# Two graph attention layers: layer 0's context as three fp32r products of split parts, and a new order of the mixed phase

## The chip, the cores and the metric

The kernel runs on one core of a Trainium2 chip. The metric is the device time of one launch, in microseconds. The core has five engines with an instruction list each: TensorE (PE, matrix products; its weight loads are shown as PEld), VectorE (DVE), ScalarE (ACT), GpSimd (POOL) and SyncE (SP, which here issues all DMAs). Every engine follows its own list strictly in order and waits on semaphores; while one instruction waits, all that stand behind it on that engine wait as well.

## The reference, cut to what matters

There are 16 graphs of N = 512 nodes with D = 256 channels. `x` is (16, 512, 256), `adj` is (16, 512, 512) with entries 0 and 1. Two layers follow each other.

Layer 0 has one head of width 256:

```
q = x @ Wq + bq;  k = x @ Wk + bk
scores = q k^T / 16, -1e18 where adj == 0
attn = softmax(scores), 0 where adj == 0
ctx = (attn @ x) @ Wc
x = layer_norm(x + ctx) * gamma + beta
```

Layer 1 has 8 heads of width 32, and the logarithm of the clipped adjacency is added to its scores (the kernel multiplies the exponentials by the clipped adjacency instead, which is the same):

```
logits = q k^T / sqrt(32) + log(clip(adj, 1e-8))
out = softmax(logits) @ v, heads joined, @ Wo^T + bo
x = layer_norm(x + out) * gamma + beta
```

All is in float32. The kernel keeps that accuracy in two ways: with matrix products of type fp32, or by splitting each operand into a high part (fp32r, a rounded form) and a low part (the rest), and adding up the three products high by high, high by low and low by high in fp32r.

## The kernel before, in words

**Tiles.** A graph has T = 4 row tiles of 128 nodes and C = 2 halves of the channels. Layer 1's eight heads form GROUPS = 2 groups of four; its 32 score tiles of 128x512 are handled as 8 quads (quad = 4*group + row tile) of two pairs of heads each.

**Phases.** The work is a software pipeline over the graphs. One pass of the loop, a "mixed phase", does three things at once: the front of graph j (layer 0, and layer 1's projections and row maxima), the back of graph i = j-1 (layer 1's attention), and the tail of graph t = i-1 (output projection, second norm, store). `run` (L424) issues a first phase (front only), one phase without a tail, 14 full phases as a loop over i from 1 to 14, then a last phase (no front) and an end (tail only).

**Order.** Inside a phase the order is written out by hand as a list of stages: FIRST, SCHEDULE (the mixed phases) and LAST, L61 to L115. Each engine walks the same list (`follow`) and does its own part of each stage that it knows, so the list fixes the order on all engines. A stage in the list such as ("scores1", 2, 1) makes TensorE compute two score tiles, ScalarE take their exponentials, and GpSimd multiply the pair by the clipped adjacency (L1146), unless ("mask", 2, 1) is in the list: then VectorE does this multiplication (L991) where "mask" stands.

**Banks.** Four PSUM banks ("misc") serve the stages in MISC_DRAIN in turn. The stage that fills a bank waits until the stage four uses earlier has been drained, by ScalarE or by VectorE as the table says. Two further banks hold layer 1's scores, one its summed values (PV), one its denominators (DEN); the last two also hold the output projection. Layer 1's weights have three SBUF buffers `PR`, so quad n's exponentials wait until quad n-3 has been summed.

**The stages that matter here**, with the lines of the profile:
- split: ScalarE casts the transposed x to its high part XTH (L806), VectorE subtracts (XTL, L954).
- q0: six matmuls (L600), ScalarE writes Q0H (L811), VectorE Q0L (L970). q1 and k1 likewise, for layer 1.
- u: rows of x @ Wc, six fp32r matmuls of 258 columns (L610); ScalarE copies them to U (L822).
- bias: VectorE makes the 0/1 array ABSENT from the adjacency (L983). max0: a row bound of layer 0's scores, matmuls L652 and L654, VectorE reduces (L995). floor, shift0: ScalarE and VectorE turn this into the shift NM0 (L827, L1001, L834).
- scores0: eight matmuls of 512 columns (L665, L669, L670), then ScalarE's exponential into P0 (L838).
- context0: per tile four fp32 matmuls of P0 by U, 257 columns (L678); VectorE divides by the sum in column 0, adds x and takes statistics (L1022 to L1030). stats0: GpSimd computes 1/std (L1135, L1137). norm0: VectorE writes xn (L1045). transpose: L687, parts XNH (ScalarE, L873) and XNL (VectorE, L964). v: L622, copied by ScalarE (L816). residual: two GpSimd operations (L1129, L1131).
- max1 (g, n): one 32-row matmul (L700) and one VectorE reduction of 128x512 (L1006), 16 for each group. mrow1 (g): TensorE turns the 16 columns of maxima (L705), VectorE copies (L1012), and a DMA puts them into the stacks QS. clip: L979.
- scores1 (L721), values1 and denominators1 (L744), sums_v, sums_w (ScalarE, L857, L863), reciprocal (L1053), normalise (L1059), high_output (ScalarE, L868), low_output (L1063), and project (24 matmuls, L766; VectorE adds the residual, L1072). The projection's first tile has its four products with the high part first and waits for low_output of group 1 only before its sixth matmul. stats1, norm1, output: VectorE L1078 to L1088, GpSimd L1135, L1137, L1160, L1162.

SP copies the parts of q1 and k1 into the stacks, 24 DMAs for each group, and issues the loads for the next graph between them; it is a queue in order as well.

## Time and profile before

| | |
|---|---|
| time, median of 3 runs | 1230.44 us (1230.1 to 1231.08) |
| time of the profiled execution | 1230.28 us |
| its span, first to last instruction | 1228.5 us |
| its mean granted TensorE clock | 0.974 |
| busy share TensorE, VectorE, GpSimd, ScalarE | 93%, 76%, 60%, 43% |

The span is what the profile's views divide up; the time has 1.8 us around it. Times in the rows are microseconds from the start of the span unless marked ns. In the order-of-time views, matmuls in a row are merged: "x8" is eight records, and the length given is that of the merged row. Ends of matmuls are modelled and overlap what follows, so a stage's cost is read from its start to the start of the next stage. A matmul of type fp32 leaves two records. An entry in brackets is the idle time of the engine ahead of the row and what ended it.

### The profile page before, as it was taken

The page shows a single profiled execution, that of the slowest core. Times are in us where ns is not written, and L with a number is a line of the kernel's source. Part 1 is how long each engine was busy: PE and PEld are TensorE (multiplying, and loading weights), DVE is VectorE, ACT ScalarE, POOL GpSimd, SP SyncE. Part 2 cuts the span into 40 slices and gives each one's busy share as a digit, 9 for nine tenths or more (in the row PEclk, how much of TensorE's full clock was granted, in tenths as well). Part 3 has the DMA queues.
Part 4 walks back from the last instruction along what each step waited for, and adds up shares of the span by engine and source line. Part 5 has one row for each costly group of instructions (what it writes and reads, how often), then busy time and mean ns, then how long its engine had stood idle before and what let it go on. Part 6 is the DMA issues. An engine that isn't in the chain of part 4 may idle for free.

```text
span 1228.5 us, 21300 instructions
## 1 busy us (share of the span) xinstructions
PE 1148.0 (93%) x6474; PEld 686.1 (56%) x6474; DVE 934.6 (76%) x1735; ACT 523.5 (43%) x1020; POOL 734.1 (60%) x352
## 2 busy tenths in 40 slices
PE   6879999999999999999999999999999999999883
PEld 5656465655646565564656556465656646565431
DVE  4465887968778796877879687887968788796874
ACT  1224454444345444434544443444444344444431
POOL 0007568474956847485784748577474857757462
...
GB/s 129 0 115 58 66 107 39 137 32 123 66 85 87 43 140 23 126 62 92 79 45 143 17 128 60 96 80 44 140 17 131 57 100 86 37 137 17 87 34 17
DMA packets 69652, 94.67 MB, mean 77 GB/s; under 512 B 14081, under 2 KB 32769, under 8 KB 69634
## 3 DMA queue, kind: packets, MB, share of 16 engines
...
q14 instruction: 8, 0.07, 0.0%
...
## 4 chain that ended last, share of the span: by engine, by line
PE 40%; DVE 23%; POOL 18%; issue 12%; ACT 5%; DMA 1%; DVEq 0%; POOLq 0%; ACTq 0%; SPq 0%
PE misc L600 11%; DVE mx L1006 8%; POOL PR L1146 8%; PE scores L721 6%; PE misc L622 4%; PE misc L610 3%; POOL z L1160 3%; POOL res L1129 3%; PE misc L652 2%; PE misc L700 2%; DVE PR L991 2%; PE values L744 2%; PE values L766 2%; DVE K1L L970 2%; DVE sums_w L1053 2%
## 5 line engine op out<-in xcount | busy, mean ns | idle before, releaser
L1146 POOL TENSOR_TENSOR PR<-PR,CLIP 128x1024 f32<-128x1024 f32 x217 | 543.0, 2527 | 373.3 <-ACT PR L850 373.3
L1006 DVE TENSOR_REDUCE mx<-misc 128x1 f32<-128x512 f32 x512 | 322.6, 681 | 92.9 <-PE misc L700 92.6
L850 ACT ACTIVATE PR<-scores 128x512 f32<-128x512 f32 x512 | 279.3, 602 | 226.5 <-PE scores L721 217.9
L721 PE MATMUL scores<-QS,KS 97*128 97x512 f32 x512 | 196.4, 461 | 8.9 <-issue 3.5
L744 PE MATMUL values<-PR,V 128*32 128x512 f32 x1024 | 133.2, 604 | 14.5 <-DVE PR L991 14.4
L744 PE MATMUL denominators<-PR,ones 128*32 128x512 f32 x1024 | 133.7, 605 | 0.8 <-DVE z L1072 0.3
L721 PEld LDWEIGHTS scores<-QS,KS 97*128 97x128 f32 x512 | 89.7, 193 | 68.1 <-ACT PR L850 36.1
L700 PE MATMUL misc<-K1H,Q1H 32*128 32x512 f32 x512 | 119.7, 502 | 6.4 <-DVE K1L L970 1.6
L678 PE MATMUL misc<-U,P 128*128 128x257 f32 x512 | 121.8, 386 | 0.0
L1053 DVE RECIPROCAL sums_w<-sums_w 128x128 f32<-128x128 f32 x128 | 114.1, 925 | 6.9 <-ACT sums_w L863 4.0
L700 PEld LDWEIGHTS misc<-K1H,Q1H 32*128 32x128 f32 x512 | 48.4, 184 | 119.1 <-DVE mx L1006 63.7
L678 PEld LDWEIGHTS misc<-U,P 128*128 128x128 f32 x512 | 94.6, 189 | 19.8 <-issue 3.8
L838 ACT ACTIVATE P<-misc 128x512 f32<-128x512 f32 x64 | 38.3, 598 | 96.3 <-PE misc L670 96.3
L744 PEld LDWEIGHTS values<-PR,V 128*32 128x32 f32 x1024 | 25.2, 109 | 68.9 <-issue 44.6
L991 DVE TENSOR_TENSOR PR<-PR,CLIP 128x1024 f32<-128x1024 f32 x39 | 59.8, 1538 | 1.9 <-ACT PR L850 1.8
L665 PE MATMUL misc<-Q0H,XTH 128*128 128x512 f32 x128 | 59.0, 461 | 0.0
L816 ACT COPY V<-misc 128x512 f32<-128x512 f32 x32 | 18.7, 585 | 89.5 <-PE misc L622 89.5
L1135 POOL TENSOR_TENSOR ve<-mv,eps 128x4 f32<-128x4 f32 x32 | 6.4, 202 | 83.0 <-DVE mv L1037 59.3
L1160 POOL TENSOR_TENSOR z<-z,spread 128x1024 f32<-128x1024 f32 x16 | 38.3, 2391 | 28.9 <-DVE z L1088 28.9
L970 DVE SCALAR_TENSOR_TENSOR Q1L<-misc,cols,Q1H 128x512 fp32r<-128x512 f32 x32 | 24.0, 751 | 39.8 <-ACT Q1H L811 39.8
L744 PEld LDWEIGHTS denominators<-PR,ones 128*32 128x32 f32 x1024 | 22.4, 108 | 52.6 <-issue 46.1
L665 PE MATMUL misc<-Q0L,XTH 128*128 128x512 f32 x128 | 51.0, 398 | 0.0
...
## 6 DMA issues: line engine op xcount, KB each, us to landing
...
QS<-Q1H SPq DMA_DIRECT2D x256, 64.0 KB, 2.0
KS<-K1H SPq DMA_DIRECT2D x256, 64.0 KB, 2.0
...
QS<-Q1L SPq DMA_DIRECT2D x128, 64.0 KB, 2.0
KS<-K1L SPq DMA_DIRECT2D x128, 64.0 KB, 2.0
...
```

Source lines behind the costliest of these rows:

```text
L600: mm = pe.matmul(bank[:], w[:, k, P * c:P * (c + 1)], s[:, k, :], start=(n == 0), stop=(n == len(terms) - 1))
L665: pe.matmul(bank[:], kk[:, c, rows_k], qq[:, c, :], start=(n == 0), stop=False)
L678: mm = pe.matmul(bank[:, 0:D + 1], P0[:, k, P * t:P * (t + 1)], U[:, k, 0:D + 1], start=(k == 0), stop=(k == T - 1))
L700: pe.matmul(bank[:], Q1H[part, g, P * t:P * (t + 1)], K1H[part, g, :], start=True, stop=True).then_inc(misc_filled, 1)
L721: pe.matmul(ST[n][:], KS[:, h, P * k:P * (k + 1)], QS[:, h, :], start=True, stop=True).then_inc(scores_filled, 1)
L744: mm = pe.matmul(bank[DK * h:DK * (h + 1), :], w, PR[quad % WEIGHT_BUFFERS][:, h, :], start=(k == 0), stop=(k == T - 1))
L850: act.activation(PR[quad % WEIGHT_BUFFERS][:, h, :], ST[n][:], ACT.Exp, scale=SCALE1).then_inc(exp_done, 1)
L991: dve.tensor_tensor(w, w, clipped, ALU.mult).then_inc(masked_dve, 1)
L1006: dve.tensor_reduce(mx1[:, g, h, t:t + 1], misc_bank(ph, "max1", g, n)[:], AX.X, ALU.max, negate=True).then_inc(misc_drained["dve"], 1)
L1053: dve.reciprocal(sums_w[:, q], sums_w[:, q]).then_inc(back_step, 1)
L1146: pool.tensor_tensor(w, w, clipped, ALU.mult).then_inc(masked_pool, 1)
L1160: pool.tensor_tensor(z[:], z[:], all_rows(S_G1), ALU.mult).then_inc(pool_step1, 1)
```

## The change

Layer 0's context becomes three fp32r products of high and low parts. P0H is the exponential a second time, written as fp32r by ScalarE; its low part is P0 less P0H, computed by GpSimd in a new stage low0 (two operations of 128x1024), and put where XNH and XNL lie, which are free at that time. UH is written by ScalarE in place of U, and UL by VectorE (PSUM less UH), so that the stage u is now drained by VectorE. context0 has 12 matmuls of 258 columns per tile in place of four of 257: four of P0H by UH, four of P0H by UL, four of the low weights by UH, and in the first tile two waits for GpSimd stand before the last group. The list of the mixed phase is reordered throughout; the mask of (3, 0) moves from GpSimd to VectorE. FIRST gains the two low0 stages, LAST is as it was.

```diff
 FIRST = [
...
-    ("scores0", 0), ("scores0", 1), ("prepare", 0), ("scores0", 2), ("scores0", 3), ("prepare", 1),
+    ("scores0", 0), ("scores0", 1), ("low0", 0), ("prepare", 0), ("scores0", 2), ("scores0", 3), ("low0", 1), ("prepare", 1),
...
 SCHEDULE = [
-    ("reciprocal", 1, 0), ("skip_back",), ("split", 0), ("split", 1), ("max1", 1, 0), ("reciprocal", 1, 1),
-    ("max1", 1, 1), ("q0", 0), ("q0", 1), ("scores1", 0, 0), ("bias",), ("u", 0), ("reciprocal", 1, 2),
-    ("scores1", 0, 1), ("u", 1), ("scores1", 1, 0), ("reciprocal", 1, 3), ("u", 2), ("max0", 0),
-    ("normalise", 1), ("scores1", 1, 1), ("max0", 1), ("u", 3), ("high_output", 1), ("max0", 2),
-    ("scores1", 2, 0), ("low_output", 1), ("max0", 3), ("max1", 1, 2), ("max1", 1, 3), ("scores1", 2, 1),
-    ("floor",), ("project",), ("skip_back",), ("max1", 1, 4), ("max1", 1, 5), ("shift0",), ("max1", 1, 6),
-    ("stats1",), ("max1", 1, 7), ("values1", 0), ("values1", 1), ("max1", 1, 8), ("max1", 1, 9),
-    ("denominators1", 0), ("scores0", 0), ("scores0", 1), ("skip_back",), ("output",), ("scores0", 2),
-    ("scores1", 3, 0), ("scores0", 3), ("norm1",), ("max1", 1, 10), ("residual",), ("max1", 1, 11),
-    ("max1", 1, 12), ("denominators1", 1), ("denominators1", 2), ("max1", 1, 13), ("max1", 1, 14),
-    ("max1", 1, 15), ("context0", 0), ("scores1", 3, 1), ("mrow1", 1), ("context0", 1), ("context0", 2),
-    ("scores1", 4, 0), ("values1", 2), ("scores1", 4, 1), ("mask", 4, 0), ("context0", 3),
-    ("scores1", 5, 0), ("denominators1", 3), ("sums_w", 0), ("stats0",), ("norm0",), ("reciprocal", 0, 0),
-    ("values1", 3), ("denominators1", 4), ("reciprocal", 0, 1), ("scores1", 5, 1), ("sums_v", 0),
-    ("transpose", 0), ("mask", 5, 0), ("scores1", 6, 0), ("values1", 4), ("transpose", 1),
-    ("scores1", 6, 1), ("skip_front",), ("values1", 5), ("reciprocal", 0, 2), ("reciprocal", 0, 3),
-    ("q1", 0), ("k1", 0), ("normalise", 0), ("scores1", 7, 0), ("denominators1", 5), ("max1", 0, 0),
-    ("max1", 0, 1), ("max1", 0, 2), ("scores1", 7, 1), ("q1", 1), ("high_output", 0), ("max1", 0, 3),
-    ("max1", 0, 4), ("max1", 0, 5), ("denominators1", 6), ("clip",), ("values1", 6), ("max1", 0, 6),
-    ("max1", 0, 7), ("k1", 1), ("max1", 0, 8), ("denominators1", 7), ("max1", 0, 9), ("max1", 0, 10),
-    ("values1", 7), ("max1", 0, 11), ("max1", 0, 12), ("max1", 0, 13), ("v", 0), ("max1", 0, 14),
-    ("sums_w", 1), ("max1", 0, 15), ("low_output", 0), ("v", 1), ("mrow1", 0), ("sums_v", 1),
+    ("reciprocal", 1, 0), ("split", 0), ("split", 1), ("max1", 1, 0), ("max1", 1, 1), ("max1", 1, 2),
+    ("bias",), ("q0", 0), ("reciprocal", 1, 1), ("scores1", 0, 0), ("reciprocal", 1, 2), ("u", 0),
+    ("scores1", 0, 1), ("q0", 1), ("scores1", 1, 0), ("reciprocal", 1, 3), ("u", 1), ("u", 2),
+    ("scores1", 1, 1), ("max1", 1, 3), ("normalise", 1), ("max0", 0), ("u", 3), ("high_output", 1),
+    ("scores1", 2, 0), ("max0", 1), ("max0", 2), ("low_output", 1), ("max1", 1, 4), ("max1", 1, 5),
+    ("floor",), ("max0", 3), ("project",), ("scores1", 2, 1), ("shift0",), ("skip_back",), ("stats1",),
+    ("max1", 1, 6), ("max1", 1, 7), ("max1", 1, 8), ("denominators1", 0), ("scores0", 0), ("output",),
+    ("scores0", 1), ("scores0", 2), ("denominators1", 1), ("low0", 0), ("skip_back",), ("norm1",),
+    ("values1", 0), ("max1", 1, 9), ("scores0", 3), ("max1", 1, 10), ("max1", 1, 11), ("max1", 1, 12),
+    ("scores1", 3, 0), ("max1", 1, 13), ("low0", 1), ("max1", 1, 14), ("scores1", 3, 1), ("residual",),
+    ("max1", 1, 15), ("context0", 0), ("mrow1", 1), ("context0", 1), ("skip_front",), ("values1", 1),
+    ("context0", 2), ("mask", 3, 0), ("scores1", 4, 0), ("denominators1", 2), ("scores1", 4, 1),
+    ("mask", 4, 0), ("context0", 3), ("denominators1", 3), ("stats0",), ("values1", 2), ("scores1", 5, 0),
+    ("norm0",), ("mask", 5, 0), ("sums_w", 0), ("values1", 3), ("scores1", 5, 1), ("denominators1", 4),
+    ("sums_v", 0), ("transpose", 0), ("values1", 4), ("scores1", 6, 0), ("reciprocal", 0, 0),
+    ("transpose", 1), ("scores1", 6, 1), ("values1", 5), ("reciprocal", 0, 1), ("reciprocal", 0, 2),
+    ("q1", 0), ("reciprocal", 0, 3), ("scores1", 7, 0), ("k1", 0), ("scores1", 7, 1), ("q1", 1),
+    ("denominators1", 5), ("max1", 0, 0), ("max1", 0, 1), ("denominators1", 6), ("normalise", 0),
+    ("high_output", 0), ("max1", 0, 2), ("max1", 0, 3), ("max1", 0, 4), ("max1", 0, 5),
+    ("denominators1", 7), ("max1", 0, 6), ("skip_back",), ("clip",), ("values1", 6), ("max1", 0, 7),
+    ("max1", 0, 8), ("low_output", 0), ("max1", 0, 9), ("k1", 1), ("values1", 7), ("max1", 0, 10),
+    ("sums_w", 1), ("max1", 0, 11), ("v", 0), ("max1", 0, 12), ("max1", 0, 13), ("max1", 0, 14),
+    ("max1", 0, 15), ("v", 1), ("sums_v", 1), ("mrow1", 0),
 ]
...
-    "q0": "dve", "u": "act", "max0": "dve", "scores0": "act",
+    "q0": "dve", "u": "dve", "max0": "dve", "scores0": "act",
...
-                for k in range(T):
-                    mm = pe.matmul(bank[:, 0:D + 1], P0[:, k, P * t:P * (t + 1)], U[:, k, 0:D + 1],
-                                   start=(k == 0), stop=(k == T - 1))
+                terms = [(w, u, k) for w, u in ((P0H, UH), (P0H, UL), (None, UH)) for k in range(T)]
+                for n, (w, u, k) in enumerate(terms):
+                    if t == 0 and w is None and k % 2 == 0:
+                        pe.wait_ge(weights0_low, ph.j * 2 + k // 2 + 1)
+                    q = slice(P * t, P * (t + 1))
+                    mm = pe.matmul(bank[:, 0:D + 2], w[:, k, q] if w is not None else P0L[k][:, q], u[:, k, 0:D + 2],
+                                   start=(n == 0), stop=(n == len(terms) - 1))
...
             def exp0(ph, k):
                 wait_filled(act, ph, "scores0", k)
+                act.activation(P0H[:, k, :], misc_bank(ph, "scores0", k)[:], ACT.Exp, scale=SCALE0)
                 act.activation(P0[:, k, :], misc_bank(ph, "scores0", k)[:], ACT.Exp,
                                scale=SCALE0).then_inc(misc_drained["act"], 1)
...
+            def context_rows_low(ph, t):
+                dve.wait_ge(u_high, ph.j * T + t + 1)
+                dve.tensor_tensor(UL[:, t, 1:1 + D + 2], misc_bank(ph, "u", t)[:, 0:D + 2],
+                                  UH[:, t, 1:1 + D + 2].bitcast(F32), ALU.subtract).then_inc(misc_drained["dve"], 1)
...
+            def weights_low(ph, half):
+                pool.wait_ge(misc_drained["act"], misc.count(ph, "act", "scores0", 2 * half + 1))
+                k = slice(2 * half, 2 * half + 2)
+                pool.tensor_tensor((XNH, XNL)[half][:], P0[:, k, :], P0H[:, k, :].bitcast(F32),
+                                   ALU.subtract).then_inc(weights0_low, 1)
```

## Rows read from the trace of the kernel before

**Rows 1.** The page's first part: busy time of each engine over the span.
```profile
PE 1148.0 (93%) x6474; PEld 686.1 (56%) x6474; DVE 934.6 (76%) x1735; ACT 523.5 (43%) x1020; POOL 734.1 (60%) x352
```

**Rows 2.** Stretches: start:end, length, busy time of each engine, granted clock, DMA.
```profile
604.76:676.10 71.34, 69.43 (x404) 41.46 (x400) 56.87 (x107) 32.29 (x63) 46.89 (x23) 1.00 0.29 81
643.53:655.50 11.97, 11.72 (x76) 6.17 (x68) 11.29 (x18) 3.05 (x6) 1.65 (x1) 1.00 0.68 191
655.50:669.55 14.05, 13.45 (x77) 9.85 (x77) 13.88 (x18) 9.73 (x21) 8.11 (x4) 1.00 0.41 100
```
The engines stand in the order PE, PEld, DVE, ACT, POOL.

**Rows 3.** Order of time of TensorE: start, length, engine, line, operation.
```profile
618.32 3.74 PE L678 MATMUL misc<-U,P 128*128 128x257 f32 x16
...
622.45 1.07 PE L744 MATMUL values<-PR,V 128*32 128x512 f32 x8
623.45 0.73 PE L721 MATMUL scores<-QS,KS 97*128 97x512 f32 x2
624.02 1.90 PE L678 MATMUL misc<-U,P 128*128 128x257 f32 x8
...
634.46 1.07 PE L744 MATMUL values<-PR,V 128*32 128x512 f32 x8 [0.95 <-DVE PR L991]
635.46 0.73 PE L600 MATMUL misc<-XNH,Wq_high 128*128 128x512 f32 x2
...
638.32 0.64 PE L721 MATMUL scores<-QS,KS 97*128 97x512 f32 x2
...
641.24 0.63 PE L600 MATMUL misc<-XNH,Wq_high 128*128 128x512 f32 x2
...
656.33 1.02 PE L600 MATMUL misc<-XTH,A_high 128*128 128x512 f32 x2 [0.51 <-ACT XTH L806]
...
659.51 0.63 PE L721 MATMUL scores<-QS,KS 97*128 97x512 f32 x2
...
661.76 0.41 PE L610 MATMUL misc<-Wc_high,XTH 128*128 128x258 f32 x2
...
662.49 0.68 PE L721 MATMUL scores<-QS,KS 97*128 97x512 f32 x2
...
669.44 0.40 PE L766 MATMUL values<-Wo_high,OTH 128*128 128x256 f32 x2
...
672.38 0.51 PE L700 MATMUL misc<-K1H,Q1H 32*128 32x512 f32 x4
```

**Rows 4.** Order of time of VectorE, the same columns.
```profile
629.12 1.38 DVE L1045 TENSOR_SCALAR xn<-X,mv,rstd 128x256 f32<-128x256 f32 x4 [1.41 <-POOL rstd L1137]
...
643.53 0.75 DVE L970 SCALAR_TENSOR_TENSOR Q1L<-misc,cols,Q1H 128x512 fp32r<-128x512 f32 x1 [1.07 <-ACT Q1H L811]
...
648.98 3.67 DVE L1006 TENSOR_REDUCE mx<-misc 128x1 f32<-128x512 f32 x6
...
665.52 1.22 DVE L1059 TENSOR_TENSOR sums_v<-sums_v,sums_w 128x512 f32<-128x512 f32 x1
...
667.95 1.60 DVE L1063 TENSOR_TENSOR OTL<-sums_v,OTH 128x512 fp32r<-128x512 f32 x1
```

**Rows 5.** Groups by line (busy us, mean ns); then two lines' durations (ns min/median/max).
```profile
L838 ACT ACTIVATE P<-misc 128x512 f32<-128x512 f32 x64 | 38.3, 598 | 96.3 <-PE misc L670 96.3
L964 DVE TENSOR_TENSOR XNL<-misc,XNH 128x512 fp32r<-128x512 f32 x32 | 21.0, 657 | 1.3 <-ACT XNH L873 1.3
L991 DVE TENSOR_TENSOR PR<-PR,CLIP x39: 1161/1226/3155, 124.1 to 1201.0; 128x1024 f32<-128x1024 f32 x39
L1059 DVE TENSOR_TENSOR sums_v<-sums_v,sums_w x32: 676/683/1237, 140.5 to 1208.8; 128x512 f32<-128x512 f32 x32
```

**Rows 6.** Order of time of GpSimd.
```profile
605.51 0.20 POOL L1135 TENSOR_TENSOR ve<-mv,eps 128x4 f32<-128x4 f32 x1 [0.42 <-DVE mv L1083]
...
613.46 2.37 POOL L1146 TENSOR_TENSOR PR<-PR,CLIP 128x1024 f32<-128x1024 f32 x1
...
661.45 12.69 POOL L1146 TENSOR_TENSOR PR<-PR,CLIP 128x1024 f32<-128x1024 f32 x5 [16.27 <-ACT PR L850]
```

22 lines of the change are left out of this document (14 added, 8 removed).

## The prediction

> **What bounds the kernel now.** I read the views in this order. The page's first part says that TensorE is busy for 93% of the span, VectorE for 76%, GpSimd for 60%, ScalarE for 43% [rows 1]. The loop repeats itself, so one mixed phase stands for all: 71.3 us, with TensorE busy 69.4 of them, VectorE 56.9, ScalarE 32.3, GpSimd 46.9, and the granted clock at 1.00 [rows 2]. Read so, TensorE is the bound and two microseconds of idle time are left. But every engine follows its list in order, so an engine with an idle share can still hold the others through a run in which it never rests. I therefore read TensorE and VectorE in order of time [rows 3, 4] and mark four points of a phase:
> - X, the first q1 matmul: 635.46.
> - VectorE starts the second q1 low part: 643.53, or X + 8.1.
> - VectorE ends low_output of group 1 (its last work before the projection): 667.95 + 1.60 = 669.55.
> - P, the first stage behind the projection: 672.38, and one period of 71.34 earlier 601.04. From there to X are 34.4 us.
>
> 8.1 + 26.0 + 2.8 + 34.4 = 71.3, the period. In the 26.0 VectorE is busy for 11.29 + 13.88 = 25.2 [rows 2]. The projection starts on TensorE at 669.44, 0.1 us before low_output ends: there both engines are the bound together.
>
> **What the change removes.** context0 is four fp32 matmuls of 257 columns per tile, each seen as two records. Two tiles and the scores1 behind them take 618.32 to 622.45; less 0.57 for the scores1 (as 623.45 to 624.02) and halved, 1.78 us a tile [rows 3]. The new form is 12 fp32r matmuls of 258 columns. Six of that kind are the stage u, 661.76 to 662.49, so 0.122 us each [rows 3]; twelve make 1.46, and with 0.07 for the change of stage 1.53. The saving is 0.25 us a tile, 1.0 a graph, 16 us over 16 graphs if TensorE alone set the time. The two new waits cost no more than 0.1 us each where the low part is there.
>
> **What it adds.** ScalarE: four more exponentials a graph, into fp32r. No row has one; the f32 one is 0.60, VectorE's 128x512 into fp32r 0.66, both as bounds [rows 5]; I take 0.65. ScalarE has 39 us free in a phase, and a scores0 tile of eight 512-column matmuls takes TensorE 1.9 (q1 0 and k1 0, twelve of them, 635.46 to 638.32), so 1.3 us of exponentials keep up. VectorE: four subtractions a graph of 128x258, PSUM less SBUF. Bounds: 0.34 us (xn, 256 columns, four in 1.38) and 0.66 (128x512 from PSUM into fp32r) [rows 4, 5]; it is half the columns of the second with a fixed part, so nearer the first: 0.37, 1.5 us a graph. One more mask, (3, 0), costs VectorE 1.2 to 1.8 us and frees GpSimd of 2.4 to 2.5 [rows 5, 6]. GpSimd gains two subtractions of 128x1024, which I price as its other operations of that size: 2.37 alone, 2.54 in a row of masks (12.69 for five) [rows 6]; I take 2.38. Sums over a phase: VectorE about 60 us, GpSimd 49, ScalarE 35, all under the period. By shares nothing stands against the saving. The order does.
>
> **The four pieces in the new order.**
> *From X to the second q1 low part.* Ahead of q1 1 stand only q1 0, scores1 (7,0), k1 0, scores1 (7,1): 2.9 us for the projections, 1.1 for the two scores1. From the start of q1 1 to its low part are 2.3 (641.24 to 643.53) [rows 3, 4]. Sum 6.3, down from 8.1.
> *VectorE's run.* Between q1 1 and low_output 1 VectorE's list holds all that it held, and in addition max1 (0,0), (0,1), (0,2), normalise 0, max1 (1,2), (1,3), and u 0 to 3. A max reduction in a row costs 0.61 us (six in 3.67) [rows 4]: five are 3.05. normalise is 0.65, the subtractions 1.5. low_output 0 no longer lies between the last max1 and mrow1, so that hand-over to TensorE and back stands open: 0.4, between none and 0.6 (one reduction). Of the 0.85 idle, 0.6 can be filled. 26.0 + 3.05 + 0.65 + 1.5 + 0.4 - 0.6 = 31.0 us. As VectorE follows its list, nothing makes this shorter but shorter instructions. The part after 655.50 grows from 14.05 to 16.8 us, to 672.3. TensorE has one scores1 less and one max1 more than in its 13.1 us from 656.33 to 669.44, and then five matmuls of the projection before it needs the low part: it is there at 669.7. So it waits there, or on the misc banks just ahead, 2.6 us a phase.
> *From low_output to P.* 19 of the projection's 24 matmuls remain, of 2.94 us: 2.3.
> *From P to the next X.* scores1 (2,1) now stands behind the projection, and GpSimd must mask it before it may do layer 1's rstd, the two operations of the output and then both low parts: scores1's start to its mask's 1.95 (659.51 to 661.45), mask 2.4, rstd to the end of the output 7.95 (605.51 to 613.46), low parts 4.75 [rows 3, 6], P + 17.1. TensorE had 14.6 us from P to context0 (618.32 less a tile, a scores1 and an mrow1); now it has two max1 and two sums stages less (2.3) and two scores1 more (1.1, with 0.6 of wait for the exponentials between them), so it is at its second wait at P + 15.2, and waits 1.9. With the last two matmuls it leaves context0's first tile at P + 17.4. From the second tile to X were 17.1 us (618.32 to 635.46). The same stages follow now, with mrow1 and two sums stages at 0.95 to 1.0 more (2.2), three tiles at 0.25 less, the 0.95 us wait for mask (5,0) at 634.46 gone since that mask stands earlier, and 0.6 less of small waits for xn: 17.0. X is at P + 34.4, as before.
>
> The sum is 6.3 + 31.0 + 2.3 + 34.4 = 74.0 us, 2.7 more than 71.3. Fourteen full phases: 38 us. The first phase has no cover for the low parts: one exponential and one subtraction more, 3.0 us, ahead of the last four products, of which 1.0 is hidden and 1.0 saved by the tiles, so +1. The phase without a tail and the last two count nothing: their tail or front is missing, and with it one side of the run. The profiled execution took 1230.28 us (span 1228.5); the median of the runs is 1230.44, 0.2 above, which I ignore. 1230.3 + 38 + 1 = **1269 us**.
> DMA: the SP queue keeps its order. The mrow of group 0 goes out later against scores1 (0,0), by up to 1 us, which stops TensorE where it is ahead of VectorE's run: nothing; 1 us if that cover were gone.
>
> **A rule against it.** A VectorE mask took up to 3.16 us for a median of 1.23, the normalise up to 1.24 for 0.68, and the long low_output above lies beside GpSimd's five masks [rows 4 to 6]. My sum carries the old lengths on. The Trainium skill (SBUF — State Buffer, Who interferes with whom) says that a VectorE instruction with two SBUF inputs and a GpSimd instruction that reads SBUF lock each other out for a whole instruction, and that one with a single SBUF input is free of it; by that the u subtractions are free, the masks and the low parts are not, and each could wait once for the other. That is rival 3.
>
> **Rivals.** (1) *TensorE stays the bound.* The place is the wait at the projection; it is won where VectorE's run takes under 31.0 - 2.7 = 28.3 us: if the subtractions hide in gaps, and normalise and low_output of group 1 fall outside GpSimd's masks (0.68 each in place of 1.22 and 1.60, 1.5 us less). Then a phase gives 1.0 us back, 16 in all, and perhaps the 0.95 of mask (5,0): 1214 us, down to 1201. For it: 69.4 of 71.3 us busy. Against: the additions to the run alone are 5.2 us. 17 in 100. (2) *No change*, within 0.2%, which is about what a measurement of this kernel can tell: 0.17 us a phase, 1230 us. 5 in 100. (3) *The lock lengthens it*: one GpSimd operation of 2.4 us in front of mask (3,0) or (5,0), on which TensorE's sums stages wait, half of it on the path: 1.2 us a phase, 1269 + 17 = 1286. For it: the 3.16 of the row. Against: both masks have 1 to 2 us of room. 7 in 100. (4) *Slower by only 3 to 15 us*, if half the waits between P and X and the open hand-over are hidden: 6 in 100. The forecast has 65 in 100, from 1245 to 1284 us (1 to 3.8 us a phase). The range from 1230 to 1288 takes in the value of rival 3 and leaves out rival 1 and what lies above rival 3, under 20 in 100. Slower: 65 + 7 + 6 = 78 in 100.
>
> **What would show it.** Right: a phase near 74 us with TensorE busy for about 68; VectorE without a gap from the second q1 low part to low_output 1, 31 us; TensorE waiting for low_output at the projection or for VectorE's drains just before, and for GpSimd's subtraction in context0's first tile; tiles near 1.5 us; the wait on mask (5,0) gone. Wrong: gaps in that run, a projection that finds its low part ready, or a phase under 71.3 us.

## The result, and the profile after

| | before | after |
|---|---|---|
| median of the runs (lowest to highest) | 1230.76 us (1230.1 to 1231.9, 4 runs) | 1280.05 us (1277.03 to 1284.58, 4 runs) |
| profiled execution, its span | 1230.28, 1228.5 us | 1284.58, 1282.8 us |
| mean granted TensorE clock of the profiled execution | 0.974 | 0.957 |

The ratio is 1.0395 (95% interval 1.0375 to 1.0415): slower, by 49 us. The forecast was 1269, its range 1230 to 1288. The profiled execution is the slowest of the four runs, 4.5 us above the median, so what follows divides up 54.3 us of span (1282.8 less 1228.5).

The page's first part for the kernel after, busy time and share of each engine:

```profile
PE 1210.5 (94%) x6730; PEld 708.5 (55%) x6730; DVE 952.5 (74%) x1815; ACT 550.9 (43%) x1084; POOL 777.6 (61%) x369
```

Stretches of it (start:end, length, busy time in the order PE, PEld, DVE, ACT, POOL, granted clock, DMA). The first two are whole periods from one X (first q1 matmul) to the next; the next three are the second of them cut at mrow1 of group 0, called M here, and at P (first stage behind the projection). Then three single microseconds inside the last of these, and the first phase from X to M:

```profile
513.57:587.25 73.68, 72.25 (x421) 41.69 (x417) 57.91 (x112) 33.95 (x67) 49.77 (x24) 1.00 0.28 79
587.25:662.29 75.04, 73.66 (x420) 42.91 (x417) 57.56 (x112) 33.95 (x67) 49.54 (x24) 0.98 0.27 77
587.25:607.37 20.12, 19.72 (x113) 10.79 (x109) 17.22 (x26) 6.57 (x12) 8.27 (x4) 1.00 0.47 144
607.37:625.85 18.48, 17.68 (x102) 12.88 (x103) 17.55 (x28) 10.29 (x22) 12.71 (x5) 1.00 0.42 100
625.85:662.29 36.44, 36.27 (x208) 19.24 (x207) 22.80 (x58) 17.09 (x34) 28.56 (x15) 0.95 0.09 29
640.00:641.00 1.00, 1.00 (x3) 0.38 (x3) 1.00 (x2) 0.88 (x3) 1.00 (x1) 1.00 0.16 51
641.00:642.00 1.00, 1.00 (x5) 0.84 (x5) 1.00 (x3) 0.46 (x1) 1.00 (x1) 0.62 0.00 0
642.00:643.00 1.00, 1.00 (x7) 1.00 (x6) 0.29 (x1) 0.00 (x0) 1.00 (x2) 0.50 0.00 0
62.69:89.66 26.97, 22.10 (x65) 14.65 (x65) 13.89 (x21) 3.33 (x5) 0.00 (x0) 0.63 0.39 117
```

The same first stretch of the kernel before was shorter and had a higher clock:

```profile
62.53:86.28 23.75, 18.70 (x65) 11.98 (x65) 13.89 (x21) 3.40 (x6) 0.00 (x0) 0.77 0.44 131
```

Two things are to be seen. The period [rows 2: 71.34] is now 73.5 to 73.7 us in five of the fourteen full phases and 74.9 to 75.5 in nine, and the nine differ by one event: behind P the granted clock falls to 0.50, the lower level of 1.2 GHz, for some 3 us. No phase of the kernel before has that. And the first phase lost 3.2 us between X and M, with the clock at 0.63 for 0.77.

| piece of a phase, us | before | after |
|---|---|---|
| X to M | 19.15 | 20.05 |
| M to P | 17.81 | 18.48 |
| P to X | 34.41 | 35.10, or 36.4 with the clock's fall |
| period | 71.37 | 73.64, or 74.95 |

| where 54.3 us of span went | us |
|---|---|
| 14 full phases at 2.28 each | 31.9 |
| nine falls of the clock at 1.35 | 12.2 |
| from the first X to the second (78.34 for 73.48) | 4.9 |
| ahead of the first X | 0.2 |
| from the last X to the end (98.59 for 93.44) | 5.1 |

TensorE's busy time rose by 62 us. Little of that can be work: `order_only` below issues the very instructions of the kernel before in another order, and its page says 1211.8 us for their 1148.0 [rows 1]. A matmul that waits in the pipeline, and one at the lower clock, count as busy.

VectorE of the kernel after in order of time, from M to the projection (start, length, what, and the idle time ahead):

```profile
607.80 0.28 DVE L1030 CAST nm<-misc 16x128 fp32r<-16x128 f32 x1 [0.56 <-PE misc L716]
...
616.67 0.36 DVE L1024 TENSOR_TENSOR UL<-misc,UH 128x258 fp32r<-128x258 f32 x1
...
618.46 0.69 DVE L1024 TENSOR_TENSOR UL<-misc,UH 128x258 fp32r<-128x258 f32 x2
...
619.67 0.74 DVE L1077 TENSOR_TENSOR sums_v<-sums_v,sums_w 128x512 f32<-128x512 f32 x1
...
620.93 0.41 DVE L1024 TENSOR_TENSOR UL<-misc,UH 128x258 fp32r<-128x258 f32 x1
...
622.46 0.74 DVE L1081 TENSOR_TENSOR OTL<-sums_v,OTH 128x512 fp32r<-128x512 f32 x1
```

GpSimd meanwhile: the masks under the two VectorE operations of L1077 and L1081, and then the two low parts:

```profile
617.48 2.38 POOL L1164 TENSOR_TENSOR PR<-PR,CLIP 128x1024 f32<-128x1024 f32 x1
619.81 2.84 POOL L1164 TENSOR_TENSOR PR<-PR,CLIP 128x1024 f32<-128x1024 f32 x1
...
637.45 2.38 POOL L1169 TENSOR_TENSOR XNH<-P,P0H 128x1024 fp32r<-128x1024 f32 x1
639.79 2.36 POOL L1169 TENSOR_TENSOR XNL<-P,P0H 128x1024 fp32r<-128x1024 f32 x1
```

VectorE's long run is there, with 1.1 us of idle time in it (0.31, 0.56 and 0.25, at mrow1 and just ahead of it): it starts the second q1 low part at 593.39 (X + 6.14) and ends low_output of group 1 at 622.46 + 0.74 = 623.20, 29.8 us later. The two operations that stretch under GpSimd's masks, normalise and low_output, take 0.74 each here and took 1.22 and 1.60 before [rows 4].

### The profile page after: what moved, and what is told of

It is laid out like the page before. It is cut to its first block, busy times and chain, and to the rows that moved or that the text cites. A ratio compares the mean times of both kernels' runs of the same rounds, so it can differ in the third digit from the quotient of the medians.

```text
span 1282.8 us, 22073 instructions
## 1 busy us (share of the span) xinstructions
PE 1210.5 (94%) x6730; PEld 708.5 (55%) x6730; DVE 952.5 (74%) x1815; ACT 550.9 (43%) x1084; POOL 777.6 (61%) x369
## 4 chain that ended last, share of the span: by engine, by line
PE 72%; DVE 15%; issue 9%; ACT 2%; DVEq 1%; DMA 1%; POOL 0%; POOLq 0%; SPq 0%; ACTq 0%
PE scores L732 9%; PE misc L606 9%; PE values L755 8%; PE misc L689 8%; DVE mx L1019 8%; PE denominators L755 8%; PE misc L671 7%; PE misc L711 5%; PE misc L658 3%; PE misc L628 2%; PE values L777 2%; PE denominators L777 2%; DVE sums_w L1071 2%; PE misc L616 1%; DVE Q0L L983 1%
## 5 line engine op out<-in xcount | busy, mean ns | idle before, releaser
L1164 POOL TENSOR_TENSOR PR<-PR,CLIP 128x1024 f32<-128x1024 f32 x202 | 511.6, 2556 | 393.1 <-ACT PR L862 384.0
L711 PE MATMUL misc<-K1H,Q1H 32*128 32x512 f32 x512 | 149.4, 506 | 9.4 <-issue 2.7
L711 PEld LDWEIGHTS misc<-K1H,Q1H 32*128 32x128 f32 x512 | 61.6, 185 | 142.2 <-DVE mx L1019 69.5
L849 ACT ACTIVATE P0H<-misc 128x512 fp32r<-128x512 f32 x64 | 38.3, 598 | 103.9 <-PE misc L676 103.9
L1169 POOL TENSOR_TENSOR XNH<-P,P0H 128x1024 fp32r<-128x1024 f32 x16 | 38.0, 2377 | 40.8 <-ACT P L850 40.8
L822 ACT ACTIVATE K1H<-misc,cols 128x512 fp32r<-128x512 f32 x32 | 22.0, 688 | 79.8 <-PE misc L606 79.8
L689 PEld LDWEIGHTS misc<-UH,P0H 128*128 128x128 f32 x256 | 39.3, 207 | 22.9 <-DVE X L1044 12.6
L671 PE MATMUL misc<-Q0H,XTL 128*128 128x512 f32 x128 | 50.9, 398 | 0.0
L689 PE MATMUL misc<-UH,P0H 128*128 128x258 f32 x256 | 50.2, 322 | 0.0
L658 PE MATMUL misc<-XTH,Q0H 128*128 128x512 f32 x128 | 44.4, 428 | 4.5 <-DVE Q0L L983 4.3
```

The costliest lines, as they stand in the source:

```text
L658: pe.matmul(bank[:], Q0H[:, c, q], XTH[:, c, :], start=(c == 0), stop=False)
L671: pe.matmul(bank[:], kk[:, c, rows_k], qq[:, c, :], start=(n == 0), stop=False)
L689: mm = pe.matmul(bank[:, 0:D + 2], w[:, k, q] if w is not None else P0L[k][:, q], u[:, k, 0:D + 2], start=(n == 0), stop=(n == len(terms) ...
L711: pe.matmul(bank[:], Q1H[part, g, P * t:P * (t + 1)], K1H[part, g, :], start=True, stop=True).then_inc(misc_filled, 1)
L1164: pool.tensor_tensor(w, w, clipped, ALU.mult).then_inc(masked_pool, 1)
```

## The experiments

Three theories stood at the start, and the expectations name them. **A, the order:** the new list makes VectorE's run longer and puts the low parts late, and the arithmetic is nearly free. **B, the arithmetic:** the subtractions, or the waits for the low parts, cost the time. **C, the clock:** the falls of TensorE's clock are most of it. The exclusive lock between VectorE and GpSimd, rival 3 of the prediction, is a fourth; `swap_norm` tests it. Twelve kernels tell them apart. The number of clock falls is counted in each kernel's profiled execution. Ratios are against the kernel before, with the 95% interval.

**1. The new order with the old arithmetic** (`order_only`). The kernel before with the new SCHEDULE less its two low0 stages:

```diff
-    ("reciprocal", 1, 0), ("skip_back",), ("split", 0), ("split", 1), ("max1", 1, 0), ("reciprocal", 1, 1),
+    ("reciprocal", 1, 0), ("split", 0), ("split", 1), ("max1", 1, 0), ("max1", 1, 1), ("max1", 1, 2),
...
```

> The new order with the arithmetic of before (four fp32 matmuls, u drained by ScalarE, no low0). Theory A (the order is what costs: VectorE's in-order run and the bare stretch before context0): without four subtractions (1.4 us) in the run and with tiles 1.0 us dearer a phase, a loop phase of 73.0 to 74.5 us and 1255 to 1280 us. Theory B (the added arithmetic costs, whatever the order): 1225 to 1235 us. Theory C (dips of TensorE's clock are most of it, and come with the short fp32r matmuls behind a stretch of waits): no dip in the loop, a phase near 73.0, 1255 us.

Measured: 1280.8 us, 1.0412 [1.0387, 1.0437]. One period of it, then its part from context0 to X and the one ahead of it, from P to context0. Below them the same two parts of the kernel before, the one from P to context0 first:

```profile
587.54:661.88 74.34, 73.21 (x404) 41.77 (x401) 57.58 (x108) 32.09 (x63) 44.38 (x22) 1.00 0.28 78
...
641.06:661.88 20.82, 20.81 (x119) 10.15 (x119) 14.02 (x36) 8.79 (x17) 15.29 (x8) 1.00 0.00 0
625.82:641.06 15.24, 15.13 (x74) 7.89 (x73) 8.79 (x24) 6.46 (x14) 8.32 (x5) 1.00 0.20 69
```

```profile
601.04:615.59 14.55, 14.55 (x88) 7.47 (x87) 9.19 (x24) 4.65 (x10) 12.14 (x7) 1.00 0.21 64
615.59:635.46 19.87, 18.91 (x108) 10.41 (x105) 14.94 (x36) 9.55 (x18) 15.35 (x9) 1.00 0.03 10
```

The order alone costs all of it: 3.0 us a phase (X to M 0.9, M to P 0.4, P to X 1.6). Against this kernel the new arithmetic takes 0.94 off P to X (36.04 to 35.10) and adds 0.23 to M to P (18.25 to 18.48): 0.7 us a phase won. The kernel after needs the same 1280 us all the same: its clock falls in nine phases and here in three (7 us more), and its stretches ahead of the second X and behind the last are 6 us longer. The period of 74.3 is what theory A gave (73.0 to 74.5), and the time is at the upper end of its range (1255 to 1280). B and C fail, C because the phase without a fall is already 3.0 us longer.

**2. The new arithmetic in the old order** (`arith_only`). The kernel after with the old SCHEDULE, in which

```diff
-    ("output",), ("scores0", 2), ("scores1", 3, 0), ("scores0", 3), ("norm1",),
+    ("output",), ("low0", 0), ("scores0", 2), ("scores1", 3, 0), ("scores0", 3), ("low0", 1), ("norm1",),
```

> The new arithmetic in the order of before; low0 stands just before scores0 2 and just behind scores0 3, mask (3,0) stays with GpSimd. Theory A: the subtractions lengthen VectorE's run to the projection by 1.4 us where it has no slack, the tiles give 1.0 back, and the low parts come some 1 to 1.5 us late behind the output's two operations: a phase of 72 to 73 us, 1240 to 1255 us. Theory B: as the whole change, 1270 to 1285 us. Theory C: TensorE's saving shows, 1214 to 1225 us.

Measured: 1334.23 us, 1.0831 [1.081, 1.0851], 78.5 us a phase. TensorE's wait in the first tile, and VectorE's normalise and low_output:

```profile
671.98 0.80 PE L688 MATMUL misc<-UH,XNL 128*128 128x258 f32 x2 [3.47 <-POOL XNL L1168]
```

```profile
644.66 2.60 DVE L1076 TENSOR_TENSOR sums_v<-sums_v,sums_w 128x512 f32<-128x512 f32 x1
...
648.71 1.32 DVE L1080 TENSOR_TENSOR OTL<-sums_v,OTH 128x512 fp32r<-128x512 f32 x1
```

None of the three theories had this. The arithmetic is not free by nature: in the old list it costs 7 us a phase, 3.2 or 2.0 of them from M to P and 4.0 or 5.3 from P to X. The second low part comes 3.47 us late, since both stand behind the output's two operations on GpSimd and a mask of 2.37 lies between them; normalise stretches from 1.22 to 2.60; and the clock falls to 0.50 once or twice in every phase. What the new order does for this arithmetic is worth more than what it costs; it had to be changed, and the changed one is still slower than the old pair.

**3. Without the weights' low parts** (`no_low0`), **4. without the subtraction for UL** (`no_u_low`).

```diff
-                    if t == 0 and w is None and k % 2 == 0:
-                        pe.wait_ge(weights0_low, ph.j * 2 + k // 2 + 1)
-                    mm = pe.matmul(bank[:, 0:D + 2], w[:, k, q] if w is not None else P0L[k][:, q], u[:, k, 0:D + 2],
+                    mm = pe.matmul(bank[:, 0:D + 2], (w if w is not None else P0H)[:, k, q], u[:, k, 0:D + 2],
-                  "stats1": rstd1_of, "output": output, "low0": weights_low}
+                  "stats1": rstd1_of, "output": output}
```

```diff
-    "q0": "dve", "u": "dve",
+    "q0": "dve", "u": "act",
-                "mask": mask, "u": context_rows_low, "max0": max0,
+                "mask": mask, "max0": max0,
```

> The changed kernel with GpSimd's low0 and its two waits left out (the third four products use the high weights again, so the low parts of the weights are missing from the sum; TensorE's work is the same). Theory A as the trace now reads (the low parts land just when TensorE asks for them): within 5 us of the changed kernel, 1272 to 1282, with the dips perhaps gone or moved. If GpSimd's chain is on the path (the prediction's 1.9 us wait a phase): 1250 to 1258 us.

> The changed kernel with VectorE's four subtractions of u left out and the bank released by ScalarE (the low parts of the rows are zero; TensorE's work is the same). Theory A: VectorE's run is 1.4 us shorter and holds TensorE from the second q1 to the projection, so a phase is 1.0 to 1.4 us shorter: 1260 to 1268 us. Rival (TensorE's own work and the clock set the time): within 4 us of the changed kernel.

`no_low0` leaves the low parts of the weights out of the sum and `no_u_low` those of the rows; TensorE's work stays. Measured: `no_low0` 1273.66 us, 1.0346 [1.0323, 1.0369]; P to X is 34.97, so the whole GpSimd chain and TensorE's two waits hold 0.13 us of a phase. `no_u_low` 1267.51 us, 1.0293 [1.0276, 1.031]; M to P is 18.22. Each is faster than the kernel after mostly because the clock falls less often: in three and two phases of the profiled execution for nine. With no_u_low a phase without a fall is 73.46 for 73.64: 7 x 1.35 + 14 x 0.18 = 12.0 us, and the fourteen phases are 12.1 shorter. Its 1267.5 us lie in the range that theory A gave, but not for theory A's reason, which was a phase shorter by 1.0 to 1.4. The four subtractions hold 1.45 us of VectorE's run, and taking them away shortened M to P by 0.25 and the end of low_output, counted from M, by nothing: 618.68 - 602.85 = 15.83, in the kernel after 623.20 - 607.37 = 15.83. VectorE's rows say why, and GpSimd's beside them:

```profile
614.12 1.77 DVE L1077 TENSOR_TENSOR sums_v<-sums_v,sums_w 128x512 f32<-128x512 f32 x1
...
617.61 1.07 DVE L1081 TENSOR_TENSOR OTL<-sums_v,OTH 128x512 fp32r<-128x512 f32 x1
```

```profile
612.94 2.40 POOL L1164 TENSOR_TENSOR PR<-PR,CLIP 128x1024 f32<-128x1024 f32 x1
615.29 2.83 POOL L1164 TENSOR_TENSOR PR<-PR,CLIP 128x1024 f32<-128x1024 f32 x1
```

What was taken off in front came back as stretch: 1.77 and 1.07 for 0.74 and 0.74. Both end 0.55 us behind the end of the mask that they began in (612.94 + 2.40 = 615.34, and 615.89; 615.29 + 2.83 = 618.12, and 618.68).

**5. normalise and one reduction exchanged** (`swap_norm`). To test the lock by itself, two VectorE operations that do not depend on each other change places:

```diff
-    ("scores1", 1, 1), ("max1", 1, 3), ("normalise", 1), ("max0", 0), ("u", 3), ("high_output", 1),
+    ("scores1", 1, 1), ("normalise", 1), ("max1", 1, 3), ("max0", 0), ("u", 3), ("high_output", 1),
```

> The changed kernel with normalise 1 and max1 (1,3) swapped: the same work, VectorE's normalise starts 0.6 us earlier against GpSimd's masks. If a VectorE operation with two SBUF inputs that starts inside one of the masks ends with it (the lock): the normalise takes 1.3 to 1.4 us in place of 0.74, low_output ends up to 0.6 us later, 1280 to 1289 us. If its length has another cause: 0.74 again and within 3 us of the changed kernel.

Measured: 1301.13 us, 1.0568 [1.0548, 1.0589], so 21 us more than the kernel after for the same instructions, though the clock falls in four phases only. The direction is that of the lock; the size is well above the 1280 to 1289 expected, which had low_output 0.6 us later, not locked itself. VectorE and GpSimd of it, and TensorE at the sixth matmul of the projection:

```profile
627.22 1.33 DVE L1077 TENSOR_TENSOR sums_v<-sums_v,sums_w 128x512 f32<-128x512 f32 x1
...
631.20 2.47 DVE L1081 TENSOR_TENSOR OTL<-sums_v,OTH 128x512 fp32r<-128x512 f32 x1
```

```profile
625.60 2.40 POOL L1164 TENSOR_TENSOR PR<-PR,CLIP 128x1024 f32<-128x1024 f32 x1
...
630.75 2.37 POOL L1164 TENSOR_TENSOR PR<-PR,CLIP 128x1024 f32<-128x1024 f32 x1
```

```profile
633.73 0.38 PE L777 MATMUL values<-Wo_high,OTL 128*128 128x256 f32 x1 [1.38 <-DVE OTL L1081]
```

normalise starts one reduction earlier in the same mask and takes 0.59 longer for it; that moves low_output from 0.19 us before a mask's end to 0.45 us behind the next one's start, and it takes 2.47 in place of 0.74. 0.59 + 1.73 = 2.3, and M to P is 20.55, 2.07 more. The place of the operation against the edge of a mask decides, not its size.

Seven kernels, one phase of each, give one rule in all fourteen cases:

| kernel, operation | starts | mask, start and end | ends | behind the mask's end |
|---|---|---|---|---|
| before, normalise | 665.52 | 663.80, 666.18 | 666.74 | 0.56 |
| before, low_output | 667.95 | 666.14, 669.00 | 669.55 | 0.55 |
| after, normalise | 619.67 | 617.48, 619.86 | 620.41 | 0.55 |
| after, low_output | 622.46 | 619.81, 622.65 | 623.20 | 0.55 |
| no_u_low, normalise | 614.12 | 612.94, 615.34 | 615.89 | 0.55 |
| no_u_low, low_output | 617.61 | 615.29, 618.12 | 618.68 | 0.56 |
| swap_norm, normalise | 627.22 | 625.60, 628.00 | 628.55 | 0.55 |
| swap_norm, low_output | 631.20 | 630.75, 633.12 | 633.67 | 0.55 |
| arith_only, normalise | 644.66 | 644.30, 646.71 | 647.26 | 0.55 |
| arith_only, low_output | 648.71 | 646.65, 649.49 | 650.03 | 0.54 |
| repair, normalise | 641.46 | 641.11, 643.50 | 644.04 | 0.54 |
| repair, low_output | 644.73 | 643.45, 646.25 | 646.80 | 0.55 |
| mix, normalise | 620.09 | 617.98, 620.37 | 620.92 | 0.55 |
| mix, low_output | 622.98 | 620.34, 623.18 | 623.73 | 0.55 |

The table is no choice of good cases. In the traces of all fourteen kernels normalise or low_output begins under a 128x1024 operation of GpSimd 459 times; 458 of them end 0.54 to 0.57 us behind it, one 0.63. The operations that begin under none take 0.67 to 0.69. So the length is what is left of GpSimd's operation, plus the 0.68 of its own, less 0.13. VectorE's own masks of 128x1024 do the same: 1.21 us alone, and 1.08 to 1.09 behind the end (once 1.12) where they begin under one.

The GpSimd operation that follows a blocked normalise or low_output is long in its turn: 2.79 to 2.87 us in all 322 cases of the full phases, for 2.37 to 2.41 of the masks of the table that follow none. Each such meeting costs GpSimd 0.45 us as well.

**6. The old third part of the list** (`old_s3`). From q1 0 on, the list of before; `skip_back` goes back to second place:

```diff
-    ("reciprocal", 1, 0), ("split", 0), ("split", 1),
+    ("reciprocal", 1, 0), ("skip_back",), ("split", 0), ("split", 1),
...
-    ("q1", 0), ("reciprocal", 0, 3), ("scores1", 7, 0), ("k1", 0), ("scores1", 7, 1), ("q1", 1),
+    ("reciprocal", 0, 3), ("q1", 0), ("k1", 0), ("normalise", 0), ("scores1", 7, 0), ("denominators1", 5),
+    ("max1", 0, 0), ("max1", 0, 1), ("max1", 0, 2), ("scores1", 7, 1), ("q1", 1), ("high_output", 0),
```

> The changed kernel with the last part of its list, from q1 0 to mrow1 0, in the order of before (max1 (0,0) to (0,2) again ahead of q1 1; one skip_back stands at the phase's start so that the banks keep their turn). Theory A: TensorE's time from X to mrow1 0 falls from 20.05 to 19.1 us, the rest stays: 13 to 15 us less, 1263 to 1270 us (dips may come or go, 1.4 us each). Rival (the parts trade against each other and the period is set elsewhere): 1278 to 1284 us.

Measured: 1261.09 us, 1.0237 [1.0202, 1.0272]. X to M is 19.08, 0.95 less, the other pieces are as in the kernel after: 72.65 a phase, as expected. This third of the new order is a plain loss, and the pieces add up: it can be changed by itself.

**7. The bare stretch ahead of context0 filled** (`fill`).

```diff
-    ("scores1", 3, 0), ("max1", 1, 13), ("low0", 1), ("max1", 1, 14), ("scores1", 3, 1), ("residual",),
-    ("max1", 1, 15), ("context0", 0), ("mrow1", 1), ("context0", 1), ("skip_front",), ("values1", 1),
-    ("context0", 2), ("mask", 3, 0), ("scores1", 4, 0), ("denominators1", 2), ("scores1", 4, 1),
+    ("scores1", 3, 0), ("max1", 1, 13), ("low0", 1), ("max1", 1, 14), ("denominators1", 2),
+    ("scores1", 3, 1), ("residual",), ("max1", 1, 15), ("values1", 1), ("context0", 0), ("mrow1", 1),
+    ("context0", 1), ("skip_front",), ("context0", 2), ("mask", 3, 0), ("scores1", 4, 0), ("scores1", 4, 1),
```

> The changed kernel with denominators1 2 put between scores1 (3,0) and scores1 (3,1) and values1 1 put ahead of context0 0, where TensorE waits for exponentials and max reductions, often for 0.3 to 0.8 us each. Nothing else changes. If that bare stretch costs the time and brings the clock's dips: from P to X 0.8 us less in every phase and no dip in the loop, 1255 to 1265 us. If the dips come from something else they stay: 1266 to 1272 us. If neither matters: 1278 to 1283 us.

Measured: 1275.73 us, 1.0367 [1.0337, 1.0396]. P to X of one phase of it:

```profile
622.24:658.04 35.80, 34.97 (x207) 18.01 (x206) 23.14 (x58) 17.12 (x34) 28.83 (x15) 1.00 0.09 29
```

P to X is 0.7 longer than in the kernel after without a fall of the clock (0.8 less was expected): TensorE stands 0.46 us for an exponential at a scores1 and 0.24 for a DMA. The clock does not fall in any of the fourteen phases. 14 x 0.7 = 10 lost and 12 won; in the profiled executions the parts ahead of the second X and behind the last are 7.6 us shorter as well. The median is 4 us lower, with the intervals overlapping. This may mean that the fall hangs on what TensorE does ahead of context0, but it does not show it: with that stretch unchanged the clock fell in nine phases (after), four (old_s3 and swap_norm), three (no_low0), two (no_u_low) and one (s21_first, below), each in one execution. In the kernel after that is a stretch of single scores1 and max1 stages in which the weight loads wait by turns for exponentials and reductions.

**8. scores1 (2, 1) ahead of the projection again** (`s21_first`).

```diff
-    ("floor",), ("max0", 3), ("project",), ("scores1", 2, 1), ("shift0",), ("skip_back",), ("stats1",),
+    ("scores1", 2, 1), ("floor",), ("max0", 3), ("project",), ("shift0",), ("skip_back",), ("stats1",),
```

> The changed kernel with scores1 (2,1) ahead of the projection, as before the change. The prediction's account (GpSimd's chain behind that mask delays the low parts): 0.6 to 1.5 us a phase less, 1260 to 1272 us. What no_low0 showed (the low parts land when they are asked for and cost 0.14 us): within 4 us of the changed kernel.

Measured: 1275.85 us, 1.0363 [1.033, 1.0396]: M to P 19.04 (0.56 more), P to X 34.87 (0.24 less), one fall of the clock. The move costs 0.56 ahead of P and gives back only 0.24 behind it. GpSimd's chain to the low parts, which this starts earlier, was not on the path, as no_low0 says too.

**9 to 12. Four attempts at a better order.** All four have a list of their own.

- repair: the old list, with low0 on both sides of scores0 3, mask (3, 0) on VectorE, scores1 (3, 1) and values1 2 ahead of context0, and low_output earlier;
- better1: the old list, with the reciprocals, normalise and low_output of group 1 ahead of GpSimd's masks, max1 (1, 0) to (1, 3) behind the projection, and the weights' low parts computed by VectorE;
- better0: the order of better1 with the old arithmetic;
- mix: the old list up to the projection with normalise ahead of max0 0, the new one from there to q1 0, the old one behind it.

The core of each against the old list, in this order (better0 has better1's):

```diff
-("scores1", 1, 1), ("max0", 1), ("u", 3), ("high_output", 1), ("max0", 2), ("scores1", 2, 0), ("low_output", 1),
+("scores1", 1, 1), ("high_output", 1), ("max0", 1), ("low_output", 1), ("u", 3), ("max0", 2), ("scores1", 2, 0),
...
-("reciprocal", 1, 0), ("skip_back",), ("split", 0), ("split", 1), ("max1", 1, 0), ("reciprocal", 1, 1), ("max1", 1, 1),
+("reciprocal", 1, 0), ("skip_back",), ("split", 0), ("split", 1), ("reciprocal", 1, 1), ("reciprocal", 1, 2),
+("reciprocal", 1, 3), ("normalise", 1), ("q0", 0), ("high_output", 1), ("low_output", 1), ("q0", 1),
...
-("u", 2), ("max0", 0), ("normalise", 1), ("scores1", 1, 1),
+("u", 2), ("normalise", 1), ("max0", 0), ("scores1", 1, 1),
```

> The new arithmetic on the order of before, mended where the run with the arithmetic alone lost: low0 0 and 1 directly around scores0 3 with mask (3,0) on VectorE, scores1 (3,1) and values1 2 ahead of context0, high_output and low_output of group 1 ahead of u 3, max0 2. If the arithmetic's 1.0 us a phase can be had with the right order: 70.3 to 71.5 us a phase, 1216 to 1233 us. If VectorE's four subtractions bind in any order: 72 to 73 us, 1240 to 1255 us.

> The new arithmetic in an order built from what the runs showed, on the list of before: the four reciprocals, normalise and low_output of group 1 ahead of GpSimd's first mask (no lock, and TensorE finds them done at the projection), max1 (1,0) to (1,3) behind the projection where VectorE idles, both low parts of the weights on VectorE there too, scores1 (3,1) and values1 2 ahead of context0; from q1 0 on as before. If the lock and the run to the projection were the cause of the 1334 us of the two earlier kernels with the old order: normalise and low_output at 0.7 us each and 70.0 to 71.5 us a phase, 1212 to 1233 us. If TensorE loses it elsewhere: over 1240 us.

> The same order as the kernel before it, with the arithmetic of before (fp32 matmuls of context0, u drained by ScalarE, no low parts). TensorE has 1.0 us more a phase, VectorE 3.8 us less. If TensorE's work decides under this order: 1.0 us a phase above its sibling, 14 us. If VectorE's run decides: below its sibling. Against the kernel before it shows what the order alone gives: 1215 to 1235 us.

> The new arithmetic with the list in three parts, each from the order in which that part was quickest: up to the projection as before the change, but with normalise 1 moved one reduction ahead (in the run with the old order it began just behind a mask's start and took 2.6 us); from there to q1 0 as changed; from q1 0 on as before the change. If the lock cost the old order its time with the new arithmetic: normalise near 0.7 us, from mrow1 0 to P 17.3 to 17.9 us in place of 19.8 to 21.0, a phase of 71.3 to 72.2, 1230 to 1245 us. If the subtractions of u are what costs there, whatever the masks do: 19 us and more for that part, 1255 us and above.

Measured: repair 1334.94 us, 1.0846 [1.0815, 1.0876]; better1 1312.5, 1.0672 [1.0654, 1.069]; better0 1317.31, 1.0713 [1.0695, 1.0731]; mix 1280.21, 1.0398 [1.0375, 1.042]. None is faster than the kernel before, and all four miss what was hoped for. repair and better0 lie far above all that was expected (up to 1255 and 1235), better1 in its other branch (over 1240, if TensorE loses it elsewhere). mix lies where it was to be if the subtractions of u cost the time (1255 and above), but not for that reason, as its pieces below show.

repair's P to X is 35.99 with no late low part, but normalise takes 2.58 and low_output 2.07 (the table above), M to P is 23.1 to 24.1, with a fall of the clock in every phase, and TensorE waits 2.00 us for the subtraction into UL, which stands behind low_output on VectorE. In better1 no mask is running at normalise and low_output, and they take 0.69 each; TensorE waits instead for ScalarE (1.36 for the split, 1.74 for the exponential), and P to X is 37.85. With its pair better0 it says once more what the arithmetic is worth when the order is held, here with the weights' low parts on VectorE: 38.27 - 37.85 = 0.4 us a phase, 5 us in all.

mix is the test of the lock reading on the new arithmetic in the old front part. One period of it, and VectorE's rows:

```profile
367.10:440.22 73.12, 70.90 (x420) 41.60 (x416) 57.55 (x112) 34.20 (x67) 49.61 (x24) 1.00 0.29 79
```

```profile
620.09 0.83 DVE L1077 TENSOR_TENSOR sums_v<-sums_v,sums_w 128x512 f32<-128x512 f32 x1
...
622.98 0.75 DVE L1081 TENSOR_TENSOR OTL<-sums_v,OTH 128x512 fp32r<-128x512 f32 x1
```

M to P is 17.81, as in the kernel before, with four more subtractions in it; in arith_only, where these two operations take 2.60 and 1.32, it was 19.7 to 21.1. X to M is 19.05. So two of the three pieces can hold the new arithmetic at no cost. The third did not: P to X is 36.3, and 37.85 in eleven phases with a fall of the clock, 1.2 more than in the kernel after from nearly the same list (max1 (1, 4) and (1, 5) stand in it too, scores1 (2, 1) does not). One wait of it is seen, 0.95 us for a reduction right behind the projection; the rest was not taken apart.

## Why the prediction was right, point by point

| piece | forecast | after |
|---|---|---|
| X to the second q1 low part | 6.3 | 6.14 |
| VectorE's run to low_output of group 1 | 31.0 | 29.81 |
| low_output to P | 2.3 | 2.65 |
| P to X | 34.4 | 35.10, or 36.44 |
| period | 74.0 | 73.7, or 75.0 |
| 14 phases; first; last | 38; 1; 0 | 44; 5; 5 |

**The direction held, the main reading in part.** The new order costs more than the fp32r products give, as `order_only` shows (3.0 lost, 0.7 won), and VectorE's work from X to P is the longer for what was moved into it. Putting back the old third gives 0.95 us of it back (old_s3), and low_output 2.3 us later makes M to P 2.07 longer (swap_norm). But the forecast had 2.7 us a phase between X and P and nothing behind P. The runs have 1.6 between X and P (38.53 for 36.96) and 0.7 behind it: 2.3 in all, and 3.1 with the clock's falls. And one of the signs that the prediction gave for being wrong is in the rows, a projection that finds its low part ready.

**Prices that held.** The subtraction into UL is 0.36 to 0.41 us in the rows above (forecast 0.37). ScalarE's exponential into fp32r has the mean of the f32 one [rows 5], 598 ns, where I took 650. GpSimd's low part is 2.377 us on the mean (2.38). From the page's groups:

```profile
L849 ACT ACTIVATE P0H<-misc 128x512 fp32r<-128x512 f32 x64 | 38.3, 598 | 103.9 <-PE misc L676 103.9
...
L1169 POOL TENSOR_TENSOR XNH<-P,P0H 128x1024 fp32r<-128x1024 f32 x16 | 38.0, 2377 | 40.8 <-ACT P L850 40.8
```

A tile of context0 is, from TensorE in order of time in a phase without a fall of the clock (P at 552.14), 571.05 - 569.42 = 1.63 us, as the first is, and 1.54 and 1.53 for the last two (forecast 1.53). The saving over order_only is 0.94 a graph from P to X (1.0):

```profile
567.47 0.74 PE L689 MATMUL misc<-UH,P0H 128*128 128x258 f32 x4
568.05 0.65 PE L689 MATMUL misc<-UL,P0H 128*128 128x258 f32 x4
568.53 0.40 PE L689 MATMUL misc<-UH,XNH 128*128 128x258 f32 x2
568.77 0.40 PE L689 MATMUL misc<-UH,XNL 128*128 128x258 f32 x2
569.10 0.39 PE L716 MATMUL misc<-ident,mx 128*16 128x128 f32 x2
569.42 0.74 PE L689 MATMUL misc<-UH,P0H 128*128 128x258 f32 x4
...
571.05 0.64 PE L755 MATMUL values<-PR,V 128*32 128x512 f32 x4
```

**VectorE's run, 31.0 for 29.8.** The step that was off carried the old lengths of normalise and low_output into the new order: 1.22 + 1.60 became 0.74 + 0.74, 1.34 us less. The added work itself was sized well (the hand-over at mrow1 was 0.56 for 0.4). That the two lengths shrank is an accident of the new list: swap_norm shows them at 1.33 and 2.47. Rival 3 named the lock, and put it on the masks of (3, 0) and (5, 0). There it showed no such price. In the loop of before, the mask of (5, 0) began under GpSimd's work in every phase and took 1.77 us; in the kernel after, all three VectorE masks take 1.21 to 1.22, but for (3, 0) in the five phases without a fall of the clock, 1.64 to 1.66. The line of all of them, with durations in ns (min/median/max):

```profile
L1004 DVE TENSOR_TENSOR PR<-PR,CLIP x54: 1162/1218/3156, 128.9 to 1254.4; 128x1024 f32<-128x1024 f32 x54
```

The lock's real place was the one that my sum took as fixed. The Trainium skill (SBUF — State Buffer, Who interferes with whom) has a VectorE operation with two SBUF inputs and a GpSimd operation that reads SBUF exclude each other for a whole instruction, and one with a single SBUF input, outside the two-port modes, go free. The rows agree with both halves: the fourteen cases of the table, but for the 0.13 us by which the two overlap, and the UL subtractions of 0.36 to 0.41 under the same masks. As it happens the new list puts both operations within 0.2 us of a mask's end.

**TensorE's wait of 2.6 us at the projection** is not in the rows: low_output ends at 623.20 and the first products with a low part start at 623.50, in step with those before them. The prediction allowed for waits on the banks just ahead; they are small, the largest 0.35 us, and M to P grew by 0.7 only:

```profile
617.92 0.71 PE L658 MATMUL misc<-XTH,Q0H 128*128 128x512 f32 x2 [0.35 <-DVE Q0L L983]
...
623.50 0.40 PE L777 MATMUL values<-Wo_high,OTL 128*128 128x256 f32 x2
```

**P to X.** I had the low parts at P + 17.1, TensorE at its second wait at P + 15.2 and a wait of 1.9. In the phase of P = 552.14 GpSimd ends the second part at 568.46, P + 16.3; TensorE comes to the low products at P + 16.4 (568.53) and its second wait stands at P + 16.6: it waits for nothing. The step that failed is TensorE's way to context0, 15.33 us for a forecast 14.0 (before: 14.55). From the start of each stage to the start of the next, against the phase of P = 601.04 before:

| P to context0, us | before | after | forecast change |
|---|---|---|---|
| max1 (12 in four places; 10 in five) | 1.74 | 2.37 | |
| sums stages (5; 3) | 4.70 | 2.85 | -2.3 with max1 |
| scores1 (1; 3) | 0.66 | 2.29 | +1.7 |
| four scores0 | 7.45 | 7.82 | 0 |

The max1 stages are the miss: a place with one or two costs 0.43 to 0.50 us, a place with three or four 0.43 to 0.57, so that two fewer in one place more save nothing. The first tile is left at P + 17.0 (569.10; forecast 17.4) all the same, but from there to X it takes 18.15 us where I had 17.0. mrow1 and the two sums stages add the 2.2 forecast. The tiles and scores1 stages give 1.2 where I had 1.7 (the last scores1 ahead of X still takes 1.00 for some 0.57), and of the 0.6 that I took off at the transposes nothing is seen. The wait for mask (5, 0), 0.95 us [rows 3], is gone as forecast.

**What the sum did not have** is the clock. [Rows 2] showed 1.00 in the loop and I let it stand. Between the 39 us forecast and the 54.3 lie three sums: the fourteen phases without the falls came to 31.9 for 38, the nine falls add 12.2, and the first and last parts add 10 where I had 1. That the time fell into the range is in part luck: 21 of the 54 us come from terms that the sum did not have or had at 1, and it was 6 too high in the loop. The list of the last phase did not change at all, yet its part from the last X to the end was 98.59, against 94.40 in fill with the same lists. Of these 4.2 us, 3.0 lie behind the last P (60.60 for 57.59), where both have the same mean granted clock of 0.75. So the clock's mean does not explain them, and the cause stays open.
